# Spreading the norm rows by a matmul with ones, and reordering the prologue of a gated cross-attention kernel

## What is computed

```python
q = rms_norm((x @ wq).reshape(B, L, 16, 128), q_norm_w)
k = rms_norm((x @ wk).reshape(B, L, 4, 128), k_norm_w)
k_ctx = rms_norm((h_ctx_kv @ wk_ctx).reshape(B, T, 4, 128), k_norm_w)
q = q * cos + rotate_half(q) * sin
k = k * cos + rotate_half(k) * sin
probs = softmax(q @ concat([k_ctx, k]) / sqrt(128) + mask)
out = (probs @ concat([v_ctx, v])) @ wo
# around it
x = x + tanh(g_xattn) * attention(layernorm(x), ctx, ...)
x = x + tanh(g_ffn) * ffn(layernorm(x), ...)
```

## Time and profile before

| what | value |
|---|---|
| median of 3 runs | 315.86 us (315.81 to 316.04) |
| device time of the profiled execution | 316.0 us |
| its span | 314.0 us |
| busy in the span: TensorE, VectorE, ScalarE, GpSimd | 95%, 73%, 74%, 58% |
| mean granted TensorE clock | 1.00 of full speed |

### The profile page before, as it was taken

How to read it: one execution, slowest core, us unless ns; L and a number is a source line. 1 busy time by engine, 2 the same in 40 slices (tenths; PEclk the granted TensorE clock), 3 DMA queues, 4 the chain that set the end, 5 groups by cost and what they waited for, 6 DMA issues and landing times.

```text
span 314.0 us, 6534 instructions
## 1 busy us (share of the span) xinstructions
PE 296.9 (95%) x2223; PEld 233.1 (74%) x2223; DVE 229.0 (73%) x478; ACT 232.0 (74%) x892; POOL 182.3 (58%) x177
## 2 busy tenths in 40 slices
PE   7897989998999899999999999999999999987976
PEld 3344656666767678878888888888888888786864
DVE  1668998889759976769887787758765865576554
ACT  2468688777878678897999768896888678776622
POOL 1235685577646877346975586457755684456230
PEclk9999999999999999999999999999999999999999
DMA  6999000000000010000100010000000000000001
GB/s 197 395 390 380 8 17 2 0 1 11 8 2 2 0 35 2 0 0 3 34 2 0 2 37 0 2 1 20 0 3 0 2 18 3 0 2 17 2 0 35
DMA packets 6721, 12.84 MB, mean 41 GB/s; under 512 B 801, under 2 KB 4257, under 8 KB 6689
## 3 DMA queue, kind: packets, MB, share of 16 engines
q1 hardware_dynamic: 6688, 12.43, 11.1%
HBM read 11.38 MB, written 1.05 MB: 40 GB/s over the span
## 4 chain that ended last, share of the span: by engine, by line
PE 35%; ACT 25%; DVE 22%; issue 8%; POOL 6%; DMA 2%; SPq 1%; DVEq 0%; POOLq 0%
ACT probs L897 9%; ACT squares L739 6%; PE ps_y L437 5%; DVE row_max L1168 4%; PE ps_attn L708 3%; DVE exp_bias L1171 3%; PE ps_scores L664 3%; PE ps_transposed L423 3%; DVE q_sin L1039 3%; PE ps_q L411 3%; ACT qt L817 3%; PE ps_ff L525 3%; PE ps_probs L423 2%; DVE q_rot L1035 2%; PE ps_kv L411 2%
## 5 line engine op out<-in xcount | busy, mean ns | idle before, releaser
L897 ACT ACTIVATE probs<-ps_scores,exp_bias,q_scale 128x128 f32<-128x128 f32 x128 | 56.9, 455 | 24.1 <-DVE exp_bias L1171 24.1
L1343 POOL TENSOR_TENSOR q_rot<-q_rot,q_sin 128x512 f32<-128x512 f32 x31 | 39.7, 1279 | 19.1 <-DVE q_sin L1039 18.9
L1387 POOL TENSOR_TENSOR probs<-probs,row_inv 128x512 f32<-128x512 f32 x32 | 36.7, 1146 | 17.9 <-DVE row_inv L1221 17.7
L1294 POOL TENSOR_TENSOR q_scale<-ssq_eps,minus_half 128x4 f32<-128x4 f32 x32 | 40.2, 1255 | 9.7 <-DVE ssq_eps L1194 8.9
L1305 POOL TENSOR_TENSOR fuse_lo<-fuse,fuse_hi 128x256 fp32r<-128x256 f32 x21 | 15.4, 732 | 44.1 <-ACT fuse_hi L748 44.1
L739 ACT ACTIVATE squares<-ps_q 128x128 bf16<-128x128 f32 x128 | 34.0, 292 | 6.7 <-PE ps_q L405 3.9
L708 PE MATMUL ps_attn<-pt,values 128*128 128x256 f32 x128 | 33.4, 383 | 0.0
L664 PE MATMUL ps_scores<-kt,qt 128*64 128x128 f32 x512 | 33.3, 273 | 0.0
L1035 DVE TENSOR_TENSOR q_rot<-ps_q,rope 128x512 f32<-128x512 f32 x31 | 21.2, 685 | 14.0 <-ACT squares L739 14.0
L873 ACT ACTIVATE pt<-ps_probs 128x512 f32<-128x512 f32 x32 | 19.2, 600 | 14.5 <-PE ps_probs L423 14.4
L664 PEld LDWEIGHTS ps_scores<-kt,qt 128*64 128x64 f32 x512 | 28.9, 137 | 0.0
(11 more groups left out here) (173 smaller groups left out, 824.0 us busy)
## 6 DMA issues: line engine op xcount, KB each, us to landing
q_raw<-in_wq_dram SPq DMA_DIRECT2D x4, 512.0 KB, 8.7
o_raw<-in_wo_dram SPq DMA_DIRECT2D x4, 512.0 KB, 11.5
ctx_t<-in_ctx_dram SPq DMA_DIRECT2D x8, 128.0 KB, 2.9
out_dram<-x_sb SPq DMA_DIRECT2D x8, 128.0 KB, 2.1
stage<-in_gate_w_dram SPq DMA_DIRECT2D x2, 384.0 KB, 10.5
stage<-in_up_w_dram SPq DMA_DIRECT2D x2, 384.0 KB, 11.4
x_sb<-in_x_dram SPq DMA_DIRECT2D x1, 768.0 KB, 13.4
stage<-in_down_w_dram SPq DMA_DIRECT2D x2, 384.0 KB, 13.0
```

What stands on the lines that cost most here:

```text
L897: last = nc.scalar.activation(probs[:, i, :], ps_s[:, i * P:(i + 1) * P], ACT.Exp, bias=exp_bias[:, i:i + 1], scale=q_scale[:, k % 2, i:i ...
L1294: return nc.gpsimd.tensor_tensor(dst, src, minus_half[:, 0:src.shape[1]], ALU.pow)
L1343: nc.gpsimd.tensor_tensor(q_rot[:, :, :], q_rot[:, :, :], q_sin[:, :, :], ALU.add)\
L1387: nc.gpsimd.tensor_tensor(probs[:, :, :], probs[:, :, :], row_inv[:, :].unsqueeze(2).broadcast_to([P, 4, P]), ALU.mult).then_inc(probs_rea ...
```

## The change

- The DMA of the norm rows now writes one partition: `norm_row`, 1 x 512. GpSimd sets `ones_row` (1 x 128) to one by a third memset.
- TensorE multiplies `ones_row` by `norm_row` between the two key projections: one float32 matmul with one contraction row, 128 output rows and 512 columns, into bank `ps_probs`. It waits for `rows_in` and `row_ones_set`.
- `tables()` is split. `rope_table(n)` makes one table, from `const` and `ps_probs`; the four calls now stand in `first_keys_and_queries` after the first `k_var`, in the order 2, 3, 0, 1. `mask_tables()` makes `mask` and `ident_bf` after `normalize(1)`.
- The first rotated keys are summed by GpSimd, in `first_roots` after the second `k_inv`. VectorE computes the two products of the queries before it takes `kn`, and the sum of the queries after it.
- TensorE waits for the four tables before the token values, which overwrite `ps_probs`.

```diff
-            sp.dma_start(rope[:, :, :].rearrange("p a n -> p (a n)"),
-                         norm_rows.rearrange("(a n) -> a n", a=1).broadcast_to([P, 4 * DIM])).then_inc(rows_in, 16)
+            sp.dma_start(norm_row[:, :], norm_rows.rearrange("(a n) -> a n", a=1)).then_inc(rows_in, 16)
...
                 keys_values(0, -4)
+                pe.wait_ge(rows_in, 16)
+                pe.wait_ge(row_ones_set, 1)
+                nc.tensor.matmul(ps_p[:, :], ones_row[:, :], norm_row[:, :], start=True, stop=True).then_inc(rows_spread, 1)
                 keys_values(0, -3)
...
+                pe.wait_ge(tables_ready, 4)
                 keys_values(0, -1)
...
-            def tables():
+            def rope_table(n):
+
                 dve.wait_ge(const_in, 16)
+                dve.wait_ge(rows_spread, 1)
+                col = C_COS if n % 2 == 0 else C_SIN
+                nc.vector.tensor_tensor(rope[:, n, :], const[:, col:col + DIM], ps_p[:, n * DIM:(n + 1) * DIM], ALU.mult)\
+                    .then_inc(tables_ready, 1)
...
+                for n in (2, 3, 0, 1):
+                    rope_table(n)
                 dve.wait_ge(kc_inv_ready, 1)
...
-                dve.wait_ge(ks_roped, 1)
-                nc.vector.tensor_tensor(k_cos[:, :, :], k_cos[:, :, :], k_sin[:, :, :], ALU.add).then_inc(ks_added, 1)
...
             normalize(0)
-            tables()
             first_keys_and_queries()
             normalize(1)
+            mask_tables()
...
                 inverse_root(k_inv[:, :], k_var[:, :]).then_inc(ks_inv_ready, 1)
+                pool.wait_ge(ks_roped, 1)
+                nc.gpsimd.tensor_tensor(k_cos[:, :, :], k_cos[:, :, :], k_sin[:, :, :], ALU.add).then_inc(ks_added, 1)
...
             nc.gpsimd.memset(minus_half[:, :], -0.5).then_inc(half_set, 1)
+            nc.gpsimd.memset(ones_row[:, :], 1.0).then_inc(row_ones_set, 1)
```

More of the change, by code:

```diff
@@ L113, in build @@
         rope = sb("rope", [P, 4, DIM])
+        norm_row = sb("norm_row", [1, 4 * DIM])
+        ones_row = sb("ones_row", [1, P])
         small = sb("small", [P, S_ALL])
@@ L203, in build @@
         half_set = sem("half_set")
+        row_ones_set, rows_spread = sem("row_ones_set"), sem("rows_spread")
         tables_ready = sem("tables_ready")
@@ L1000, in out_of_range, with mask_tables @@
                         .then_inc(bad_ready, 1)
-            def tables():
+            def rope_table(n):
                 dve.wait_ge(const_in, 16)
+                dve.wait_ge(rows_spread, 1)
+                col = C_COS if n % 2 == 0 else C_SIN
+                nc.vector.tensor_tensor(rope[:, n, :], const[:, col:col + DIM], ps_p[:, n * DIM:(n + 1) * DIM], ALU.mult)\
+                    .then_inc(tables_ready, 1)
+            def mask_tables():
                 nc.vector.tensor_copy(mask[:, :], const[:, C_MASK:C_MASK + LEN]).then_inc(tables_ready, 1)
@@ L1006, in tables @@
                 nc.vector.tensor_copy(ident_bf[:, :], ident).then_inc(tables_ready, 1)
[L1007 to L1011, removed]
             def scales():
@@ L1263, in first_keys_and_queries @@
                     .then_inc(ks_var_ready, 1)
-                dve.wait_ge(tables_ready, 6)
+                dve.wait_ge(tables_ready, 4)
                 nc.vector.tensor_tensor(k_cos[:, :, :], four(kv_bank(0, 0, 1)), over_heads(rope[:, 2, :]), ALU.mult)
@@ L1267, in first_keys_and_queries @@
                                         halves(over_heads(rope[:, 3, :])), ALU.mult).then_inc(ks_roped, 1)
-                dve.wait_ge(ks_roped, 1)
-                nc.vector.tensor_tensor(k_cos[:, :, :], k_cos[:, :, :], k_sin[:, :, :], ALU.add).then_inc(ks_added, 1)
-                dve.wait_ge(ks_added, 1)
-                dve.wait_ge(ks_inv_ready, 1)
-                nc.vector.tensor_tensor(kn[:, :, :], k_cos[:, :, :], by_head, ALU.mult).then_inc(ks_ready, 1)
                 dve.wait_ge(q_made, 1)
@@ L1277, in first_keys_and_queries @@
                                         ALU.mult).then_inc(q_sin_ready, 1)
+                dve.wait_ge(ks_added, 1)
+                dve.wait_ge(ks_inv_ready, 1)
+                nc.vector.tensor_tensor(kn[:, :, :], k_cos[:, :, :], by_head, ALU.mult).then_inc(ks_ready, 1)
                 dve.wait_ge(q_sin_ready, 1)
```

## The result

| | median | range | runs |
|---|---|---|---|
| before | 315.86 us | 315.75 to 316.33 | 12 |
| changed | 317.22 us | 316.21 to 318.31 | 12 |

The ratio is 1.0041, with a 95% interval of 1.0028 to 1.0054: 0.4% slower. The forecast was 316.0, with a range of 315.2 to 316.9; the measured median lies above the range. The median hides what matters: the twelve times form **two groups**, six from 316.21 to 316.38 and six from 318.06 to 318.31, with nothing between. The median of 317.22 falls into that gap: no run took about that long. The profiled execution took 316.38 (span 314.5) and belongs to the lower group. The kernel before has no such pair in these runs.

A forecast was written before the change was run, and what follows sets the result against it. The prologue was taken as bound by when kn is ready: -0.52 (later start gone) + 0.61 (slower sum) = +0.1 us, so 315.86 + 0.1 gives 316.0, range 315.2 to 316.9.

The forecast's parts named there:

- The frame: Prologue: the instant kn is ready decides; some 4.6 us of gapless TensorE work follow, and earlier queries or loads buy nothing.
- the prediction's own sign: Trace check: forecast wrong if TensorE's transposes of kn start more than half a microsecond away from 15.4.
- The matmul with ones: TensorE between context and token keys: uncovered, 0.86 us, bounds 0 and 0.99; token keys end at 10.81.
- The sum on GpSimd: Sum of the first rotated keys, 13.43 to 14.70: takes 1.27 for VectorE's 0.69, handing over costs 0.61 us.
- the last of the sum: Whole execution: median is 0.14 under the profiled run, so 315.86 + 0.1 gives 316.0.
- the rivals: Slower: late norm row or held-up GpSimd sum, 0.19 together; faster: short matmul, 0.07; path elsewhere, 0.10, mostly faster.
- the late row: Norm row's DMA lands after 8.07, delaying the token keys: 316.9 or 317.3; chance 0.19 shared with a held-up GpSimd sum.

The follow-up runs named there:

- e6: Changed kernel with 128 contraction rows, 127 of them zeros, in the matmul with ones: six runs 315.76 to 316.14 us, four 317.63 to 317.91.
- e3: Changed kernel with the sum of the keys back on VectorE, kn ahead of the query products: six runs 315.22 to 316.03 us, four 317.50 to 317.95.
- e14: Changed kernel with 9 warm-up matmuls instead of 11: traced execution 318.13 us; others five 316.02 to 316.42, two 317.76 and 318.17, two 321.07 and 322.94.
- e15: Kernel before the change with 9 warm-up matmuls: traced execution 316.45 us; others six 315.77 to 316.10, three at 317.25, 317.57 and 318.18.
- e2: Changed kernel with the matmul reading a memset row of ones, norm row awaited only at the end: nine runs 316.22 to 316.40 us, one 318.07.
- e7: Changed kernel with one more GpSimd memset that waits for the norm row's DMA, to show its landing: 316.62 us.
- e8: Changed kernel with the norm row's DMA issued one place earlier, ahead of wk: seven runs 316.10 to 316.78 us, three 318.00 to 318.12.
- e11: Changed kernel with 13 warm-up matmuls instead of 11: eight runs 316.08 to 316.50 us, two at 317.19 and 317.42.
- e12: Changed kernel without the matmul, norm rows by two broadcasts, keys' sum and kn on VectorE ahead of query products: 315.63 to 317.80 us, median 316.77.
- e5: Changed kernel, norm row on ScalarE's queue, matmul with ones replacing three warm-up matmuls, keys' sum and kn on VectorE before query products: median 317.23 us.

## Why the prediction was wrong

- **The frame held for the profiled execution.** The end of `kn` decides, and 4.6 us of TensorE follow it: 4.57 in the changed kernel (15.91 to 20.48), 4.64 before. No waits on loads appeared, the earlier queries bought nothing, the tables hid under GpSimd's root, the constants landed at 8.03 for 8.1. By the prediction's own sign, though, it fails by a hair: the transposes of `kn` were to start within half a microsecond of 15.4 and started at 15.91.
- **The matmul with ones was mis-sized.** The term was 0.86, with a bound of 0.99; the token keys were complete at 11.20 where 10.81 was put down. Start to start it took 1.05, and the group behind it 1.98 instead of 1.88; 0.1 more passed in front of it. `e6` shows that this is the price of one contraction row between neighbours with 128. The Trainium skill, page "TensorE: Matmul & The Clock Gate", section "Why this matters for your kernels", gives a matmul with 32 contraction rows the time of one with 128; here one with a single row, in float32 and alone between full ones, took 0.2 more by itself and 0.4 with its surroundings. The measurement decides. The lower group is 0.4 to 0.5 us over the kernel before, not 0.1, and this term (0.39 more) accounts for the rest: in `e6`, where the matmul takes the 0.86 put down for it, the lower group lies at 315.76 to 316.14, around the forecast of 316.0. This alone would have stayed within the range.
- **The sum on GpSimd** was right: 13.86 to 15.13 for 1.27, `kn` 0.03 behind it; 0.61 was the price, `e3` gave about 0.6 back.
- **The step that failed** is the last of the sum: "The median of the runs is 0.14 under the profiled one: 315.86 + 0.1 gives **316.0**". It gives every execution the difference found for one, and so puts at nothing what the others lose. The prediction noted that the changed chain runs over TensorE from 6.25 on without cover, and charged the matmul to it, but never asked what else that stretch could lose. In the earlier trace rows it is 1.98 us of context keys; in the executions of `e14` and `e15`, where the clock hadn't risen, it is 3.78 and 3.70. The kernel before had 1.2 us of slack there (context keys 1.72 longer, transposes of `kn` only 0.52 later: its token keys' squares began 0.96 after their bank was full, and `k_var` at 10.7 was 1.3 after its input), so that the one such execution with a trace came out at 316.45 (`e15`). The change used that slack up, and its counterpart came out at 318.13 (`e14`). Half of the twelve runs at about +1.9 put the median at 317.22. None of the rivals was this; the slower one, the late row, would have ended near the measured time, but by a mechanism that `e2`, `e7` and `e8` exclude together.
- **What stays open:** why six of twelve and four of ten runs of the changed kernel are in the upper group, and one of ten in `e2`, whose TensorE program is the same up to the context keys. No trace of the changed kernel with its 11 warm-up matmuls fell into the upper group; that `e14`'s execution of 318.13 is one of its kind rests on its time, its recorded clock and its rows. A late landing of `wk_ctx` would shift the same stretch and was not tested by itself; in the traces of the changed kernel and its variants with the matmul between the projections, the context keys started between 5.97 and 6.43, and longer warm-up (`e11`) would not cure it. The number of late runs doesn't simply follow the number of warm-up matmuls either: with nine half were in the lower group, with eleven twelve of 22.

## What to carry to other kernels

In this kernel, slack between two engines was also insurance: before filling it with work, ask what the stretch does in the executions that the one trace doesn't show, and look at all single times, not the median. A matmul put into a gapless stretch cost its full length, and one with a single contraction row 0.4 us more than that; put it where the engine waits, fill it up to 128 rows, and let it lengthen the warm-up. Moving the sum from VectorE (0.69 us) to GpSimd (1.27) cost 0.6 on the path, since `kn` waited for nothing else in the meantime.

## What was not expected of the hardware

- TensorE ran at the 1.2 GHz level where the recorded clock says 1.00: the context keys of the execution of 318.13 us took 3.78 us for 1.98, most of the single matmuls 1061 ns, as under a recorded 0.50 in `e12`. The durations tell the level, the record here doesn't. The Trainium skill's page "TensorE: Matmul & The Clock Gate", section "Seeing it yourself", warns that such records can be unreliable; the trace agrees.
- Three warm-up matmuls fewer, with a one-row matmul in their place (`e5`), went with a first projection 1.2 us longer in the trace; with two more (`e11`) none of ten runs was at +1.9, against ten of 22.
- A one-row transfer in a full queue had landed 4.0 us after its issue (7.06, issued at 3.05, `e7`), 0.6 us ahead of `wk`, which was issued before it (2.58 + 5.1 = 7.68) and behind which the prediction put it. The section on the fixed cost that the prediction cites from the Trainium skill describes transfers issued by GpSimd; this one was SyncE's, and nothing was added behind `wk`.
